# Context keys and values ahead of the layer norm, and feed-forward weights loaded in twelve turns, in a four-lane transformer stack

## The reference, cut to what matters

```python
x = x + tanh(g_xattn[i]) * xattn_i(layernorm(x), ctx)   # q from layernorm(x); k, v from ctx alone
x = x + tanh(g_ffn[i])   * ffn_i(layernorm(x))
```

## Time and profile before

| | |
|---|---|
| Median of 3 runs | 3105.86 us (3104.45 to 3106.49) |
| The profiled execution's own time | 3089.66 us |
| Its span, first to last instruction | 3088.4 us |
| Instructions | 59290 |
| Busy: TensorE, VectorE, ScalarE, POOL | 89%, 74%, 53%, 28% |
| Mean granted TensorE clock | 0.959 of full speed |

### The profile page before, as it was taken

One profiled execution on the slowest core, in us unless ns is written; L12 is line 12 of the kernel. 1 busy time (PEld: TensorE's weight loads), 2 busy tenths in 40 slices (PEclk: granted clock), 3 DMA queues, 4 the chain that ended last, 5 costly groups with the idle time before them and its releaser, 6 DMA issues.

```text
span 3088.4 us, 59290 instructions
## 1 busy us (share of the span) xinstructions
PE 2758.2 (89%) x23396; PEld 2258.5 (73%) x23396; DVE 2298.9 (74%) x5466; ACT 1651.7 (53%) x3825; POOL 853.5 (28%) x1308
## 2 busy tenths in 40 slices
PE   6888989998989999995799999998999999887998
PEld 4677868787778878784677777787777777775766
DVE  7677687868787787864677676777777877755998
ACT  4456555656565555653356564655565656542444
POOL 2011111112322321111253443323232322222554
PEclk9899989999999999997899999999999999996999
DMA  5000000000011211002011211000000000000000
GB/s 173 3 20 8 16 13 15 15 13 17 19 45 47 74 47 36 20 18 54 16 47 42 71 50 47 18 24 15 12 17 10 18 11 13 6 6 30 28 30 26
DMA packets 84077, 92.04 MB, mean 30 GB/s; under 512 B 15252, under 2 KB 77208, under 8 KB 83800
## 3 DMA queue, kind: packets, MB, share of 16 engines
q1 hardware_dynamic: 75352, 59.91, 6.2%
q0 software_dynamic: 8448, 28.34, 3.2%
HBM read 65.36 MB, written 22.85 MB: 29 GB/s over the span
## 4 chain that ended last, share of the span: by engine, by line
PE 54%; DVE 31%; ACT 6%; issue 4%; POOL 2%; SPq 2%; DMA 1%; DVEq 0%; POOLq 0%; ACTq 0%
PE psum L383 13%; PE psum L353 10%; PE psum L360 10%; PE psum L417 5%; DVE tiny L724 4%; DVE big L732 3%; PE psum L531 3%; PE psum L429 3%; PE psum L376 3%; PE psum L367 2%; PE psum L373 2%; PE psum L522 2%; SPq L1631 2%; DVE bstats L691 1%; DVE tiny L762 1%
## 5 line engine op out<-in xcount | busy, mean ns | idle before, releaser
L1372 POOL TENSOR_TENSOR tiny<-tiny,minus_half 128x1 f32<-128x1 f32 x224 | 128.3, 573 | 1327.4 <-DVE tiny L695 1326.4
L383 PE MATMUL psum<-ident,big 128*128 128x128 f32 x2816 | 423.4, 287 | 79.8 <-ACT big L1200 52.5
L383 PEld LDWEIGHTS psum<-ident,big 128*128 128x128 f32 x2816 | 324.2, 146 | 150.2 <-ACT big L1200 91.6
L1200 ACT ACTIVATE big<-big 128x512 f32<-128x512 f32 x512 | 311.3, 630 | 218.2 <-DVE big L732 217.4
L724 DVE TENSOR_REDUCE tiny<-psum 128x8 f32<-128x1024 f32 x256 | 312.5, 1221 | 74.9 <-PE psum L417 70.3
L732 DVE TENSOR_TENSOR big<-psum,tiny 128x512 f32<-128x512 f32 x512 | 329.8, 686 | 8.8
L1389 POOL TENSOR_TENSOR head_keys<-big,head_rows 128x512 f32<-128x512 f32 x256 | 267.6, 1063 | 212.2 <-ACT big L1179 190.9
L417 PE MATMUL psum<-head_keys,small 64*128 64x256 f32 x2048 | 291.2, 408 | 33.6 <-ACT big L1207 17.6
L417 PEld LDWEIGHTS psum<-head_keys,small 64*128 64x128 f32 x2048 | 186.1, 191 | 88.0 <-issue 48.9
L383 PE MATMUL psum<-ident,small 128*128 128x128 f32 x1152 | 201.1, 287 | 24.8 <-ACT small L1211 8.2
L383 PEld LDWEIGHTS psum<-ident,small 128*128 128x128 f32 x1152 | 133.2, 145 | 67.3 <-ACT small L1211 17.5
(11 more groups left out here) (318 smaller groups left out, 6594.9 us busy)
## 6 DMA issues: line engine op xcount, KB each, us to landing
ctxT<-in_ctxT SPq DMA_DIRECT2D x64, 128.0 KB, 2.1
after_L_xattn<-x SPq DMA_DIRECT2D x64, 128.0 KB, 1.7
mixture_out<-spare SPq DMA_DIRECT2D x46, 128.0 KB, 1.7
x_in<-in_x SPq DMA_DIRECT2D x32, 128.0 KB, 2.1
mixture_in<-xn SPq DMA_DIRECT2D x32, 128.0 KB, 1.7
x_in<-after_L_xattn SPq DMA_DIRECT2D x32, 128.0 KB, 2.0
bx_in<-after_L_xattn SPq DMA_DIRECT2D x32, 128.0 KB, 2.0
out<-bout SPq DMA_DIRECT2D x32, 128.0 KB, 1.7
```

Of the source, the lines that this page charges most:

```text
L383: last = pe.transpose(bank[:, k * P:(k + 1) * P], src[:, k * P:(k + 1) * P], identity)
L1200: last = act.activation(flat, flat, ACT.Exp, scale=DH ** -0.5)
L1372: pool.tensor_tensor(t.tiny[:, 1:2], t.tiny[:, 0:1], m.minus_half[:], ALU.pow).then_inc(*t.pool.tell(p, f"{l}.rstd{sub}"))
```

## The change

1. **Keys and values first.** In L0, L2, L3 and in the first round of L1, TensorE computes keys (bank b) and values (bank a) before it transposes xn, in one turn, as soon as the banks are free. ScalarE copies them out before it copies xnT. The transpose of xn waits for the values' copy. The queries go to bank b instead of a, and the scores follow their copy directly. POOL does the head keys after the power and before x plus bias. A mixture tile goes between values and transpose. "self" keeps its place but orders keys, queries, values. The second round of L1 is unchanged.
2. **Twelve turns.** `sp_lora` loads the layers' weights in 12 turns: for each of the 6 layers n, one turn with the 4-bit weights, the low-rank matrix and 8 transfers of scales, behind lane 0's mix.x of pass n + 1, and one with the other 8 transfers of scales, behind lane 0's self.x of pass n + 1. The other 7 transfers follow in a last turn.
3. All order strings of both phases are written anew. No arithmetic instruction is added or removed.

```diff
 NARROW = {
-    "pe": "xnT q kv s0 T0 T1 s1 T2 T3 pv oP oT out",
+    "pe": "kv xnT q s0 T0 T1 s1 T2 T3 pv oP oT out",
...
-    "act": "xnT q k v p0 p1 eT0 eT1 p2 p3 eT2 eT3 oP oT",
+    "act": "k v xnT q p0 p1 eT0 eT1 p2 p3 eT2 eT3 oP oT",
...
-        "pool": "rstd xb " + NARROW["pool"],
+        "pool": "rstd " + NARROW["pool"] + " xb",
...
 def pe_cross(pe, m, t, p, l):
+    if l == "L0":
+        pe.wait_ge(t.loaded_c, 16 * p + 16)
+    if l == "L2":
+        pe.wait_ge(t.loaded_c, 16 * (PASSES_A + p) + 16)
+    if (p, l) != (0, "L0") and (p, l) != (0, "L2"):
+        pe.wait_ge(*t.dve.at(p + FREE[l][0], FREE[l][1]))
+    elif l == "L2":
+        pe.wait_ge(*t.dve.at(PASSES_A - 1, "route.lg"))
+    context_keys(pe, t.b, t, m.kv[l], range(KD))
+    context_values(pe, t.b, t.a, t, m.kv[l], range(KD)).then_inc(*t.pe.tell(p, f"{l}.kv"))
+    yield
+    pe.wait_ge(*t.act.at(p, f"{l}.v"))
     yield from pe_tile(pe, m, t, p, l)
     yield from pe_normed(pe, m, t, p, l)
     yield from pe_heads(pe, m, t, p, l)
...
 def pe_wide(pe, m, t, p, l):
     v = t.v_wide.rearrange("p (h d) -> p h d", h=2 * CH)
+    pe.wait_ge(*t.dve.at(p, "bit.x"))
+    context_keys(pe, t.b, t, m.kv[l], range(CH))
+    context_values(pe, t.b, t.a, t, m.kv[l], range(CH)).then_inc(*t.pe.tell(p, f"{l}.kv0"))
+    yield
+    pe.wait_ge(*t.act.at(p, f"{l}.v0"))
     yield from pe_tile(pe, m, t, p, l)
     yield from pe_normed(pe, m, t, p, l)
...
 def pool_cross(pool, m, t, p, l, src):
     yield from pool_rstd(pool, m, t, p, l)
+    yield from pool_heads(pool, m, t, p, l)
     pool.wait_ge(*t.dve.at(p, f"{l}.xn"))
...
     pool.tensor_tensor(t.x[:], src, m.out_bias[l][:], ALU.add).then_inc(*t.pool.tell(p, f"{l}.xb"))
     yield
-    yield from pool_heads(pool, m, t, p, l)
...
     for n in range(NL):
-        load(m.qw[:, n], a["L3_q"][n].rearrange("(k p) o -> p k o", p=P))
         for k in range(KD):
+            sp.wait_ge(*lanes[0].dve.at(n + 1, ("mix.x", "self.x")[k]))
+            if k == 0:
+                load(m.qw[:, n], a["L3_q"][n].rearrange("(k p) o -> p k o", p=P))
+                load(m.lb[n], a["L3_lb"][n])
             for g in range(P // GROUP):
                 load(m.group_scale[g * GROUP:(g + 1) * GROUP, n, k, :],
                      a["L3_s"][n, k * (P // GROUP) + g:k * (P // GROUP) + g + 1, :].to_broadcast([GROUP, D]))
-        load(m.lb[n], a["L3_lb"][n])
+            yield
     load(m.la, a["L3_la"].rearrange("n r d -> r n d"))
     for n in (4, 5):
         load(m.biases[n], a["L3_ffn_biases"][n:n + 1, :].to_broadcast([P, D]))
-    yield
```

More of the change, by code:

```diff
@@ L289 @@
+        "63036026475072504634162513742704635142512306457314374215752740640167213025047136510267523612"
     ),
@@ L299, in names_of_lane @@
         if tile_of(n, p, l):
-            at = stage.index((p, f"{l}.var")) + 1 if engine == "dve" else 0
+            early = {"pe": ["kv", "kv0"], "act": ["v", "v0"], "dve": ["var"], "pool": []}[engine]
+            at = max([stage.index(n) + 1 for n in [(p, f"{l}.{e}") for e in early] if n in stage], default=0)
+            if l == "self" and engine != "dve":
+                at = 0
             stage[at:at] = [(tile_of(n, p, l)[2], name) for name in tile]
@@ L366, in context_keys @@
     for j, n in enumerate(chunks):
-        pe.matmul(bank[:, j * S:(j + 1) * S], w["k"][:, n * P:(n + 1) * P], t.ctxT[:, 0, :], start=j == 0, stop=False)
+        pe.matmul(bank[:, j * S:(j + 1) * S], w["k"][:, n * P:(n + 1) * P], t.ctxT[:, 0, :],
+                  start=j == 0, stop=False)
 def context_values(pe, keys, values, t, w, chunks):
-    c0 = chunks[0] * P
-    pe.matmul(values[:, 0:len(chunks) * P], t.ctxT[:, 0, :], w["v"][:, c0:c0 + len(chunks) * P], start=True, stop=False)
+    cols = slice(chunks[0] * P, (chunks[-1] + 1) * P)
+    pe.matmul(values[:, 0:len(chunks) * P], t.ctxT[:, 0, :], w["v"][:, cols], start=True, stop=False)
     for j, n in enumerate(chunks):
@@ L409, in pe_heads @@
         if r == 0:
-            pe.wait_ge(*t.act.at(p, f"{l}.v"))
+            pe.wait_ge(*t.act.at(p, f"{l}.v" if l == "self" else f"{l}.q"))
         else:
@@ L1164, in act_tile, with act_rows, act_values @@
     yield
-def act_heads(act, m, t, p, l):
+def act_rows(act, m, t, l, name, bank, dst):
+    if l == "self":
+        return act.activation(dst[:, 0:KD, :], bank[:, 0:D].rearrange("p (k s) -> p k s", s=S), ACT.Copy)
+    for k in range(KD):
+        last = act.activation(dst[:, k, :], bank[:, k * S:(k + 1) * S], ACT.Identity,
+                              bias=m.w[f"{l}b{name}"][:, k:k + 1])
+    return last
+def act_values(act, t, bank):
+    v = t.v.rearrange("p (h d) -> p h d", h=H)
+    return act.activation(v[:, :, 0:DH], bank[:, 0:D].rearrange("p (h d) -> p h d", h=H), ACT.Copy)
+def act_heads(act, m, t, p, l):
+    if l != "self":
+        act.wait_ge(*t.pe.at(p, f"{l}.kv"))
+        act_rows(act, m, t, l, "k", t.b, t.kT).then_inc(*t.act.tell(p, f"{l}.k"))
+        yield
+        act_values(act, t, t.b if l == "self" else t.a).then_inc(*t.act.tell(p, f"{l}.v"))
+        yield
+        yield from act_tile(act, m, t, p, l)
     act.wait_ge(*t.pe.at(p, f"{l}.xnT"))
@@ L1171, in act_heads @@
     yield
-    for name, bank, dst in (("q", t.a, t.qT), ("k", t.b, t.kT)):
-        act.wait_ge(*t.pe.at(p, f"{l}.kv" if name == "k" and l != "self" else f"{l}.{name}"))
-        for k in range(KD):
-            src = bank[:, k * S:(k + 1) * S]
-            if l == "self":
-                last = act.activation(dst[:, k, :], src, ACT.Copy)
-            else:
-                last = act.activation(dst[:, k, :], src, ACT.Identity, bias=m.w[f"{l}b{name}"][:, k:k + 1])
-        last.then_inc(*t.act.tell(p, f"{l}.{name}"))
+    if l == "self":
+        act.wait_ge(*t.pe.at(p, "self.k"))
+        act_rows(act, m, t, l, "k", t.b, t.kT).then_inc(*t.act.tell(p, "self.k"))
         yield
-    v = t.v.rearrange("p (h d) -> p h d", h=H)
+    act.wait_ge(*t.pe.at(p, f"{l}.q"))
+    act_rows(act, m, t, l, "q", t.a if l == "self" else t.b, t.qT).then_inc(*t.act.tell(p, f"{l}.q"))
+    yield
     if l == "self":
-        act.wait_ge(*t.pe.at(p, f"{l}.v"))
-    act.activation(v[:, :, 0:DH], t.a[:, 0:D].rearrange("p (h d) -> p h d", h=H), ACT.Copy
-                   ).then_inc(*t.act.tell(p, f"{l}.v"))
-    yield
+        act.wait_ge(*t.pe.at(p, "self.v"))
+        act_values(act, t, t.b if l == "self" else t.a).then_inc(*t.act.tell(p, "self.v"))
+        yield
     for r in range(2):
@@ L1317, in act_lane @@
     for p in range(PASSES_A):
-        yield from act_tile(act, m, t, p, "L0")
         yield from act_heads(act, m, t, p, "L0")
```

284 lines of the change are left out of this document (138 added, 146 removed).

## The result

The changed kernel takes **2968.77 us** (median of 4 runs, 2961.49 to 2974.35), beside 3105.15 us of the kernel before on the same chip. The ratio is 0.9564, 95% interval 0.9538 to 0.9590: 136 us faster. The forecast was 3045 us, the range 3000 to 3085.

The account below looks back on a forecast made before the run. It took a nearly full TensorE queue plus one SyncE hole as the bound. Terms -45, +2, -22 and +4 make -61 us, from 3105.86 to 3045 us; range 3000 to 3085.

Parts of the forecast that it names:

- The hole: Between the layer halves, lane 0's add waits for a store behind 111 weight loads; removing it gains 45 us.
- The turns: SyncE's twelve loading turns seldom delay a due store: +2 us, bounds 0 and 50 us.
- The shorter chain: Keys and values before the norm save 2.1 us in each of 24 narrow stages, 56 us a lane with wide ones.
- Its share of 40%: Of the 56 us shorter lane chain, 40% reaches the end because TensorE is 92.6% busy: -22 us.
- The wide stages: L1, with twice the columns, saves 0.8 us of lane chain each of 8 times, 6 us.
- the forecast 165: Sign: TensorE's idle time in the two long halves falls from 189 to some 165 us.
- Busy time: Sign: TensorE's busy time stays unchanged near 2758 us.
- Contention on POOL: Head keys on POOL beside the norm cost VectorE 10 to 15 us, of which +4 us reaches the end.
- rival 5: Head keys on POOL hold VectorE's norm, making the kernel slower, 3145 to 3191 us; chance 0.05.
- Rival 3: The lane's chain sets the pace, so all 56 us come: 3011 us, or 2961 if wholly hidden; chance 0.18.
- Rival 2: TensorE's queue is full, so the shorter chain gives nothing and turns and contention cost: 3067 us; chance 0.20.
- rival 4: The twelve SyncE turns each delay a store, +50 us, with no chain gain: 3111 us, no change; chance 0.03.

Follow-up runs that it names:

- experiment 4: Four dummy ScalarE copies before the queries' copy in L0, L2, L3: changed kernel 2964.67 to 3000.39 us; kernel before with twelve turns 3044.46 to 3071.97 us.
- experiment 3: Old stages with twelve turns against changed stages, equal care for orders: written from nothing 3131.84 and 3072.15 us; given orders refined 2956.47 and 2882.93 us.
- The refined pair: Kernel before with twelve turns, and changed kernel, both with given orders refined by moving single turns up to ten places: 2956.47 and 2882.93 us.
- the fastest version: Changed kernel with POOL's head keys waiting for the stage's normed xn, and its orders refined: 2863.43 us, ratio 0.9266 to the kernel before.
- experiments 6 and 7: Changed kernel with POOL's head keys waiting for the normed xn: 2949.71 us against 2964.67; the same wait with refined orders: 2863.43 us.
- experiment 1: Kernel before with only the twelve loading turns on SyncE added: 3042.1 us against 3086.36, ratio 0.9847; on a second chip 3039.34 and 3044.46 us.
- `after_again`: The changed kernel run once more, unaltered, beside the kernel before: 2964.67 us, ratio 0.9555.
- `after_third`: The changed kernel run again, unaltered, on chip B beside the kernel before: 2937.95 us, ratio 0.9507.

## Why the prediction was wrong, step by step

- **The hole, -45 us: right.** Alone it gave 42 to 50 us, and put back it cost 34.7 us beside turns that cost some themselves, 55.1 us beside turns that cost little.
- **The turns, +2 us: too small.** The row that I used as cover, SyncE idle for 17 us ahead of the hole, says nothing about where in a pass the turns stand. Moving five of them gave 20.3 us, 1.7 us for each of the twelve: inside my bounds of 0 and 4.2, ten times the value taken. At the same granted clock it is 11 to 14 us, still some six times.
- **The shorter chain, 2.1 us a stage: right.** Of the narrow stages 3.45 us went from behind the norm (forecast 3.1), and 2.40 us net, 57.6 us a lane (forecast 50). The step from the statistics to the end of xn grew by 1.05 us: 0.72 us of it lies between the power on POOL and the start of the norm, 0.22 us is the norm's own time beside the head keys, and the rest lies ahead of the power. I had put 1.0 us of keys and values behind xn instead, so that the net came out near is in part luck. The wide stages did not give their 0.8 us each: up to the first scores it was 0.1 us.
- **Its share of 40%, -22 us: this is the step that failed.** "TensorE's work is the same, so only its 189 us of idle time can shrink", and "nearer to the full-queue end, because TensorE is 92.6% busy". By the added copies the chain's share is 1.0 to 1.7, not 0.4 (experiment 4), and the move is worth 60 to 74 us, not 22 (experiment 3). The refined pair gives a lower share: there the reading by stages has 3.4 us less for a narrow stage and 3.0 for a wide one, 106 us a lane, for 73.5 us, so 0.7. Neither is near 0.4. What failed is the busy share of TensorE as the weight, and not the bound: the idle time of the two long stretches fell from 189 to 156 us, near the forecast 165, and nothing gained by the move exceeds 189 us.

  Busy time fell too, though I had forecast it unchanged: 24.9 us, and 61 us in the fastest version, with the same products. Most of the 61 us is the granted clock. By the traces' clock records TensorE was busy at the lower level for 164 us before, 155 after and 62 in the fastest version. A transpose product follows the one before it after 109 ns at the full clock and 213 ns at the lower one (medians, before), so half of such time is lost. By this estimate the clock accounts for 51 of the 61 us, but only for 5 of the 24.9. The other 20 us are the same products in less busy time at full clock; why is not shown. Nor is it shown whether a shorter chain raises the clock or only goes with it. My reading of the share is that four lanes which pass through the engines in a fixed order each wait for their own chain, and that a queue which looks full is full of such turns. No run tests this by itself.
- **The new order: not counted.** I treated the strings as following from the stages. They are a term of their own: 28 to 42 us by the differences of experiment 3, and 85 us to be had for the old stages by refining.
- **Contention on POOL, +4 us: too small.** VectorE lost 18.6 us, forecast 10 to 15. The end lost 15 to 20 by the medians (experiments 6 and 7), not 4; at the same granted clock it is 5 to 8 and 15. That is more than I put on the end, as xn lies on the chain, but how much more is open. The mechanism of rival 5 is real, at less than half of the 45 us from which it would decide.
- **The rivals.** Rival 3, the chain sets the pace, had the mechanism right: it gave 3011 and, with everything hidden, 2961 us, and got 0.18. The measured 2969 lies between the two, but by the new orders too, which no rival counted. The Trainium skill (Perfetto Trace Analysis, Identifying the Most-Contended Engine) does not take matmul occupancy as a measure of how close TensorE is to its limit and names weight-load occupancy instead, beside the rate of arithmetic. That pointed to this rival. This trace agrees: with weight loads at 73% of the span there was room for 226 us, and in the fastest version they are at 78%. Rival 2 falls by experiment 4, rival 4 by experiment 1.

The sum as it should have read, against 3105: -47 for the hole (42 to 50 by experiment 1); -58 to -75 for 57.6 us of narrow chain at 1.0 to 1.3, the longer norms already in it. The rest of the 136, some 14 to 31 us, is the new orders and whatever the wide stages gave behind their first scores; I have not separated these two. The shares are estimates from experiment 4, so this sum is one that fits and not the only one.

## What to carry to other kernels

Where several lanes pass in a fixed order, find out what a microsecond of one lane's chain costs before weighing it by the busy share of an engine: a few dummy copies on an engine with room measure it in one run. Compare executions at the same granted clock where a difference is small: here it about halved two of them. An order written anew is a change of its own: compare stages only with orders of equal care. An instruction moved to where "nothing waits for it" can still hold another engine that is on the chain, so give it a wait if its result isn't needed yet.

## What the runs showed of the hardware

- **Chips differ in the granted clock of one and the same program.** The executions of the changed kernel had 0.966 to 0.970 in the result, 0.965 to 0.973 in `after_again` and 0.973 to 0.976 on chip B. The windows between 700 and 900 us, first in the result, then on chip B:

```profile
700.00:800.00 100.00, 88.77 (x731) 73.93 (x731) 65.52 (x190) 49.84 (x111) 29.11 (x38) 0.88 0.06 16
800.00:900.00 100.00, 86.45 (x665) 72.05 (x662) 73.69 (x184) 51.72 (x113) 23.61 (x32) 0.85 0.12 36
```

```profile
700.00:800.00 100.00, 87.42 (x810) 73.84 (x807) 75.87 (x209) 56.64 (x124) 30.89 (x41) 0.99 0.06 16
800.00:900.00 100.00, 90.57 (x784) 75.94 (x784) 81.82 (x204) 58.76 (x127) 22.20 (x31) 0.92 0.13 39
```

  At 0.88 and 0.85 of the full clock 1396 products were done in 200 us, at 0.99 and 0.92 it was 1594. `after_again` had 0.92 and 0.86 there. The changed kernel is 27 to 31 us slower in the two series with the dip, the kernel before only 12 to 16. The clock is not the whole difference: at 0.959 and 0.960 the kernel before took 3097.7 to 3100.3 us beside `after_again`, and 3084.3 to 3093.6 beside `after_third`. A ratio to the kernel before carries over between chips only to about 0.6 per cent.
- **An added wait can be a gain:** 15.0 and 19.5 us by the medians, 5 to 8 and 15 us at the same granted clock, by keeping two instructions of VectorE and POOL apart. One norm took 1.17 us beside a product of the head keys and 0.41 alone. The Trainium skill (SBUF — State Buffer, Who interferes with whom) has the two engines exclude each other there; the means of 708 and 417 ns for one and the same group agree.
